# Every second rest mask moved from VectorE to GpSimd in a two-layer graph kernel

## The reference

```python
def _L0_gnn_ref(x, adj):            # adj: 4096 x 4096 int32, sparse, x: 4096 x 128 float32
    mask = a != 0                   # a: 128 rows of adj at a time
    masked = jnp.where(mask[:, :, None], x[None, :, :], neg)
    m = jnp.max(masked, axis=1)     # maximum over each node's neighbours
    return jnp.where(has_nbr[:, None], m, 0)

def _L1_gnn_ref(input, adj, W, a):
    h = input @ W
    e = (h @ a1)[:, None] + (h @ a2)[None, :]
    e = jnp.where(e > 0, e, 0.2 * e)
    e = jnp.where(adj > 0, e, -9e15)
    return jax.nn.elu(jax.nn.softmax(e, axis=1) @ h)

h = jnp.maximum(_layernorm(x), 0.0)
x = x + _L0_gnn_ref(h, adj)
h = jnp.maximum(_layernorm(x), 0.0)
x = x + _L1_gnn_ref(h, adj, L1_gnn_W, L1_gnn_a)
```

## Time and profile before

| | |
|---|---|
| median of 3 runs | 820.05 us (819.39 to 820.45) |
| the profiled execution's own time | 820.6 us |
| span of the profile, first to last instruction | 818.8 us |
| instructions | 14902 |
| PE busy | 722.1 us (88%) |
| DVE busy | 723.9 us (88%) |
| ACT busy | 481.0 us (59%) |
| POOL busy | 277.5 us (34%) |

### The profile page before, as it was taken

How to read it: one execution, slowest core, us unless ns; L and a number is a source line. 1 busy time by engine, 2 the same in 40 slices (tenths; PEclk the granted TensorE clock), 3 DMA queues, 4 the chain that set the end, 5 groups by cost and what they waited for, 6 DMA issues and landing times.

```text
span 818.8 us, 14902 instructions
## 1 busy us (share of the span) xinstructions
PE 722.1 (88%) x5658; PEld 498.9 (61%) x5658; DVE 723.9 (88%) x1121; ACT 481.0 (59%) x594; POOL 277.5 (34%) x256
## 2 busy tenths in 40 slices
PE   1788999999999999999999997568899999999995
PEld 1344444444444444444445443467899999999995
DVE  8899889999999999999999999874678998998894
ACT  2978888988898889888988884236330110010000
POOL 0611034434444344353343443454021330331230
PEclk9999999999999999999999999569899999999998
DMA  9799777987777787777777736214034434444410
GB/s 309 245 373 355 256 215 248 295 286 224 258 248 222 230 252 242 226 233 254 243 219 239 253 107 203 87 34 134 12 144 167 150 134 155 167 134 166 143 62 14
DMA packets 62856, 162.55 MB, mean 199 GB/s; under 512 B 6400, under 2 KB 11136, under 8 KB 58688
## 3 DMA queue, kind: packets, MB, share of 16 engines
q1 hardware_dynamic: 53776, 138.75, 49.2%
q0 software_dynamic: 9008, 22.82, 11.5%
HBM read 117.51 MB, written 44.04 MB: 197 GB/s over the span
## 4 chain that ended last, share of the span: by engine, by line
PE 53%; ACT 21%; DVE 15%; issue 7%; DMA 2%; POOL 1%; ACTq 0%; DVEq 0%; SPq 0%
PE pick_ps L688 14%; PE pick_ps L542 9%; ACT edge_t L348 8%; DVE acc L811 8%; PE order_ps L688 7%; PE order_ps L523 6%; ACT depth L357 6%; ACT first L356 4%; PE key_ps L688 3%; PE flip_ps L688 3%; PE flip_ps L514 3%; PE key_ps L555 2%; DVE rest L800 2%; DMA subset_max<-keys 1%; PE key_ps L636 1%
## 5 line engine op out<-in xcount | busy, mean ns | idle before, releaser
L811 DVE TENSOR_TENSOR acc<-pick_ps,acc 128x1024 f32<-128x1024 f32 x248 | 303.1, 1222 | 27.5 <-PE pick_ps L542 21.2
L320 POOL DMA_INDIRECT found<-subset_max,entry x192 | 203.9, 1062 | 288.5 <-DVE entry L823 180.9
L1010 DVE SCALAR_TENSOR_TENSOR rest<-depth,acc,stage 128x512 f32<-128x512 f32 x256 | 201.3, 816 | 18.9 <-PE key_ps L688 1.5
L356 ACT ACTIVATE first<-order_ps,neg 128x1024 f16<-128x1024 f32 x128 | 142.8, 1115 | 61.1 <-PE order_ps L523 58.8
L357 ACT ACTIVATE depth<-order_ps,mid 128x1024 f16<-128x1024 f32 x128 | 141.8, 1108 | 0.0
L348 ACT ACTIVATE edge_t<-flip_ps 128x1024 f16<-128x1024 uint16 x128 | 131.2, 1025 | 2.8 <-PE flip_ps L514 2.8
L688 PE MATMUL pick_ps<-keys,rest 128*128 128x129 f32 x1024 | 122.1, 281 | 10.1 <-DVE left L962 6.1
L688 PEld LDWEIGHTS pick_ps<-keys,rest 128*128 128x128 f32 x1024 | 120.4, 198 | 13.0 <-issue 7.0
L523 PE MATMUL order_ps<-edge_t,order_w 128*128 128x512 f16 x256 | 79.4, 393 | 38.7 <-ACT edge_t L348 31.1
L542 PE MATMUL pick_ps<-first,h_hi 128*128 128x512 f16 x256 | 98.0, 383 | 4.5 <-DVE acc L811 4.3
L514 PEld LDWEIGHTS flip_ps<-ident_h,stage 128*128 128x128 f16 x1024 | 69.3, 100 | 49.2 <-DMA stage<-adj 13.2
(11 more groups left out here) (154 smaller groups left out, 810.8 us busy)
## 6 DMA issues: line engine op xcount, KB each, us to landing
stage<-adj SPq DMA_DIRECT2D x64, 1024.0 KB
edge_units<-edge_t SPq DMA_DIRECT2D x64, 512.0 KB
stage<-edge_units SPq DMA_DIRECT2D x32, 1024.0 KB, 4.9
subset_max<-keys POOLq DMA_DIRECT2D x12, 512.0 KB, 8.8
found<-subset_max,entry POOLq DMA_INDIRECT x192
best<-x SPq DMA_DIRECT2D x4, 512.0 KB, 6.3
subset_max<-x POOLq DMA_DIRECT2D x4, 512.0 KB, 9.0
out<-keys POOLq DMA_DIRECT2D x7, 256.0 KB, 2.8
```

Source lines behind the costliest of these rows:

```text
L320: nc.gpsimd.indirect_dma_start(found[:, n % NG, s, :], None, subset_max, bass.IndirectOffsetOnAxis(entry[:, n, s:s + 1], 0)).then_inc(gath ...
L356: nc.scalar.activation(first[:, g % 4, :], order_ps[:, :], ACT.Relu, scale=-1.0, bias=neg[:, :]).then_inc(first_ready, 1)
L811: V.tensor_tensor(acc[:, q % 2, :], pick_ps[k][:, :], acc[:, q % 2, :], ALU.max).then_inc(raised, 1)
L1010: V.scalar_tensor_tensor(out=weight[:, n % WEIGHTS, :], in0=limit[:, q % 2, :], scalar=slope[:, c:c + 1], in1=units[:, m % EDGES, k * TI:( ...
```

## The change

From mask 12 on (steps 24 and 25) every second rest mask, 12, 14, ... up to 62, is made by GpSimd: 26 of the 64. GpSimd issues the six fetches of block n and then makes mask 12+2n. It waits for `depth` of both steps and for `digest(m-3)`, as VectorE did. A semaphore of its own, `rest_pool`, counts these masks. ScalarE's `select` and TensorE's `digest` wait for the semaphore of the engine that makes the mask. VectorE leaves these masks out; its `seconds` stay where they are.

```diff
+        rest_pool = sem("rest_pool")
...
+        BY_POOL = range(12, PAIRS // 2, 2)
+        pool_rests = lambda m: len([i for i in BY_POOL if i < m])
...
                         nc.gpsimd.indirect_dma_start(found[:, n % NG, s, :], None, subset_max,
                                                      bass.IndirectOffsetOnAxis(entry[:, n, s:s + 1], 0)).then_inc(gathered[n % NG][s % 2], 16)
+                    if n < len(BY_POOL):
+                        m = BY_POOL[n]
+                        at, to = 2 * m % 4, 2 * m % RESTS
+                        pool.wait_ge(depth_ready, 2 * m + 2)
+                        pool.wait_ge(digested, 2 * (m - RESTS // 2 + 1))
+                        nc.gpsimd.tensor_scalar(rest[:, to:to + 2, :], depth[:, at:at + 2, :], MID - 1.5, None, ALU.is_lt).then_inc(rest_pool, 1)
...
-                        act.wait_ge(rest_ready, g // 2 - 1)
+                        act.wait_ge(rest_ready, g // 2 - 1 - pool_rests(g // 2 - 1))
+                        if pool_rests(g // 2 - 1):
+                            act.wait_ge(rest_pool, pool_rests(g // 2 - 1))
...
-                        pe.wait_ge(rest_ready, n + 1)
+                        if n in BY_POOL:
+                            pe.wait_ge(rest_pool, pool_rests(n + 1))
+                        else:
+                            pe.wait_ge(rest_ready, n + 1 - pool_rests(n + 1))
...
-                    if g % 2 == 0:
+                    if g % 2 == 0 and g // 2 not in BY_POOL:
                         rests(g // 2)
-                    elif g + 1 < PAIRS:
+                    if g % 2 == 1 and g + 1 < PAIRS:
                         seconds(g // 2 + 1)
```

## The result

The changed kernel takes 859.95 us (median of 4 runs, 857.17 to 860.78) beside 820.12 us before: a ratio of 1.048 with a 95% interval of 1.046 to 1.050, 39.8 us slower. The forecast was 863.

The account below looks back on a forecast made before the run. The prediction took the closed ring of ScalarE and TensorE, 3.73 us a step, as the bound: 820.6 - 0 for the relief + 42.9 for held `seconds` = 863.5, forecast as 863 us, range 819 to 890.

Parts of the forecast that it names:

- The ring: ScalarE's edges, TensorE's rank, `first` and `depth` wait for each other in turn, 3.73 us a step, without VectorE.
- the relief: 26 comparisons of 0.68 us leave VectorE, 17.7 us in all; taken as a gain of 0.
- The mask takes 5.6 us: GpSimd's time for one 2048-column mask, chosen near line 328's 1.50 us for 512 columns, its fixed part paid once.
- The loss per mask is D - 3.95: The rank behind a mask comes late by this, through held `seconds`, take and picks: 1.65 us, 26 times, 42.9 us.
- D: How long one mask takes on GpSimd, 5.6 us in the forecast.
- R + 0.47: When VectorE's next take, behind the held `seconds`, was to start: 0.47 us after the mask's end.
- R + 1.75: When TensorE's `pick(88, 1)`, which waits for that take, was to start: 1.75 us after the mask's end.
- R + 4.35: When TensorE's `rank(92)`, queued behind the picks, could start: 4.35 us after the mask's end.
- R: The moment at which GpSimd's mask 44 ends.
- The join is held for about 1 us, with slack before the rank: VectorE's `left` beside the mask waits until about 360.0, delaying its take some 1 us without making the rank late.
- the join is held as well: Rival: `left` stands until the mask's end, losing D - 2.4, 3.2 us a mask, 83 us in all: 904 us; chance 0.10.
- `seconds` in two kinds, 26 long ones: VectorE's comparison `seconds`: half at 0.68 us, 26 long ones held until 0.55 us after a mask's end.

Follow-up runs that it names:

- relief_only: The kernel before with the 26 masks made by nobody, their digests reading a small tile of zeros; 819.1 us, ratio 0.999.
- ahead: The kernel before, all masks on VectorE, with edges made one step further ahead (AHEAD 5 in place of 4); 801.7 us, ratio 0.977.
- half_mask: The changed kernel with GpSimd making only the first of the two steps of each of its masks, VectorE the second; 819.9 us, ratio 1.000.
- left_later: The changed kernel with the join `left` made one step later, behind the take that follows `seconds`; 878.6 us, ratio 1.071.
- memsets: The kernel before, all masks on VectorE, with three GpSimd memsets of a 128x2048 float16 scratch tile where the change has its mask; 839.3 us, ratio 1.023.
- name_early: after_second with VectorE's `name` made right behind its search, one step earlier; 846.4 us, ratio 1.031.
- join_alone: name_early with the join `left` moved to where `name` stood, behind the take that follows `seconds`; 865.0 us, ratio 1.056.
- no_relief: The changed kernel with GpSimd's 26 masks written to a scratch tile nobody reads, VectorE still making all 64; 865.4 us, ratio 1.055.
- after_second: The changed kernel with GpSimd starting each mask only when VectorE has made `second` of the same steps; 873.4 us, ratio 1.065.
- ahead_after: ahead together with the whole change, 26 whole masks on GpSimd; 883.8 us, ratio 1.078.
- ahead_half: ahead together with half_mask's edit, GpSimd making one of two steps of every second mask; 808.1 us, ratio 0.985.
- ahead_relief: ahead together with relief_only's edit, the 26 masks made by nobody; 816.4 us, ratio 0.996.

## Why the prediction was right, step by step

- **The ring is the bound, the relief is worth 0.** Right. relief_only gives 0.999, and ahead, which only opens the ring, takes 18.8 us off.
- **The mask takes 5.6 us.** Measured 5.36, and for 1024 columns 2.77, so 2.53 ns a column and 0.17 us fixed. The choice near line 328's rate held; the 0.24 us are 6 of the forecast's us (26 x 0.24).
- **The loss per mask is D - 3.95.** With D = 5.36 that is 1.41; four steps took 1.41 us more. R + 0.47, R + 1.75 and R + 4.35 are 386.55, 387.83 and 390.43 with R = 386.08; the rows show 386.55, 387.90 and 390.49. half_mask bears the formula out on its other side (D below 3.95, no loss), and left_later with the join moved away (1.41 in thirteen of the steps where the clock stayed up, 1.58 in one).
- **The join is held for about 1 us, with slack before the rank.** Wrong in size. It was held for 2.1 us, and made its rank 1.29 us late, so that only 0.12 us of the 1.41 were left to `seconds`. The step that failed is the scaling of the earlier trace rows: a release 0.6 us into a 1.50 us instruction was taken times four, 2.4 us. Measured, the take behind the join starts 3.70 us into the mask of 5.36 us and the join ends at 3.77, 1.59 us before the mask does. With the mask of half_mask a held join ended 1.58 us before it too: what carries over between these two is the distance from the end, not a share of the columns. The sum stayed right because both delays end at the same place, the take that can't start before the mask is over. The rival "the join is held as well" had its mechanism half right, with the join's end at 3.77 us and not at the mask's; at the end it would have cost D - 2.4, 2.96 us for each mask.
- **`seconds` in two kinds, 26 long ones.** Its end was right (0.54 us after the mask), its length not: the join had already delayed its start, so that it is 1.07 us long. Only the first mask, with no join in it, shows the long one, 3.45 us.
- **What was not foreseen.** TensorE's clock, 1.4 us at the first mask and about 1.3 us at another, and 1.0 us from that other mask's late start: together 3.7 us, which with the 6 us from D brings 42.9 to 40.3. That the forecast came so close is in part luck: these errors have opposite signs.

The Trainium skill (SBUF — State Buffer, Who interferes with whom) has two rules that bear on this. It says that a VectorE instruction in a two-port mode and a GpSimd one exclude each other for the whole instruction: every comparison and copy here agrees. It says that one with two SBUF inputs contends only with a GpSimd instruction that reads SBUF: memsets agrees, 0.27 us beside a memset and 2.39 us beside the mask; but the join ended at 3.77 of 5.36 us, not at the end.

**What stays open.** In name_early, join_alone, memsets and all four kernels with the ring open, ScalarE's `first`, VectorE's takes and the keys start up to 2.2 us after the matmuls that they wait for are recorded as over; in no_relief mostly the takes do. Between steps 24 and 127 ScalarE stood idle before a `first` or a key, and VectorE before a take, although the rows of the matmuls were over (waits of more than 0.12 us beyond the usual, without those that end with a mask):

```
kernel        ScalarE times, us   VectorE times, us
before              0    0             8   1.5
relief_only         0    0             0   0
after               0    0             1   0.2
left_later          0    0             1   0.2
after_second        0    0             1   0.2
half_mask           0    0             1   0.3
no_relief           1    0.5          17   8.7
join_alone         17    8.4          21   9.9
name_early         20   20.3          19  17.7
memsets            25   16.8          20  20.0
ahead               2    2.2          19  11.9
ahead_after        15   10.1          13  16.5
ahead_half         38   15.8          22  20.7
ahead_relief       35   15.9          40  34.7
```

VectorE, which is nearest to the bound with the ring open, stands 22.8 us longer in ahead_relief than in ahead for this alone; the kernel is 14.7 us slower. The ends of matmuls are modelled in the profile, so TensorE could really be late, or its semaphores are. The trace of ahead_relief also holds the moments at which the semaphores were raised: in the stretch shown above the digest's at 246.89, the pick's at 247.65, the rank's at 247.69, and each waiting engine starts 0.02 us behind its own. The last two are 0.04 us apart, though the rank's two matmuls come behind the pick's: in before, relief_only, half_mask and the change no rank is signalled less than 0.43 us after a pick. So the pick's matmuls had been done at least 0.39 us before they were signalled. The two signals are closer than 0.35 us 24 times in ahead_relief, and 16 to 18 times in name_early, join_alone and ahead_half. In these cases the signal is late and not only the work. Whether that is the whole delay isn't shown, nor what sets it off; the fetches and transfers stand at other times in these kernels, which is no more than a hint. It has no part in the result of the change, whose rows have 0.2 us of it.

## What to carry to other kernels

Moving an instruction to GpSimd is not free for VectorE just because their data don't meet: ask which VectorE instructions (comparison, copy, two inputs in SBUF) will start while it runs, what is queued behind each, and how long that can wait; a GpSimd instruction short enough to fit between them cost nothing here while the ring was closed. Before relieving an engine, look for the closed ring of waits: an engine that is 94% busy may still have nothing to give, and one step of running ahead took off 18.8 us, where 17.7 us of VectorE's work gone took off 0.5.

## What the runs showed of the hardware that was not expected

- A copy of 6 columns on VectorE stood for 4.42 us beside GpSimd's tensor_scalar; alone it takes 0.16 us.
- VectorE's tensor_tensor with two SBUF inputs, held by a GpSimd tensor_scalar, ended 1.58 to 1.59 us before it, whether that one took 5.36 us (the change, join_alone) or 2.79 us (half_mask), and was not held at all by a memset (0.27 us).
- The hold works the other way too: a memset that started while a held comparison still ran took 2.23 us in place of 1.81 (memsets).
- GpSimd's tensor_scalar on float16 costs 2.53 ns a column, about what the kernel before shows for float32 in the earlier trace rows (1.50 us for 512, so 2.9 with the fixed part, an estimated 2.6 without it).
- TensorE's granted clock went down for 3.4 us after idle stretches of 1.56 and 2.78 us in the change's loop, and stayed up behind 24 of 1.81 us. In left_later it went down behind eleven of 26 masks, and the mean was 0.95.
- The signals of finished matmuls came late in some kernels: in ahead_relief those of a pick and of the rank behind it were 0.04 us apart, where 0.43 us is the least in before, relief_only, half_mask and the change.
